# A three-layer field-interaction tower on one core: the first two blocks' layer-0 operands from TensorE, with a new order of the gathered rows

## The reference, cut to what matters

```python
e = jnp.stack([tbl_0[ids[:, 0]], ..., tbl_31[ids[:, 31]]], axis=1)   # 512 x 32 fields x 16
x0 = xk = e
for W in (W0, W1, W2):            # 32 x 32 x 64, then 32 x 64 x 64 twice
    xk = relu(einsum('bmd,bhd,mhk->bkd', x0, xk, W))
    outs.append(sum(xk, axis=2))
z = concatenate(outs, axis=1)
h = concatenate([z, dense_ctx], axis=1)
h = maximum(h @ W_top1 + b_top1, 0)
h = maximum(h @ W_top2 + b_top2, 0)
y = h @ W_top3
```

## Time and profile before

| | us |
|---|---|
| runs of the kernel | 358.14, 358.73, 359.80 (median 358.73) |
| the profiled execution | 356.49 |
| its span in the trace | 354.7 |
| PE busy | 294.3 (83%) |
| DVE busy | 274.4 (77%) |
| POOL busy | 255.2 (72%) |
| ACT busy | 57.2 (16%) |

### The profile page before, as it was taken

How to read it: one execution, slowest core, us unless ns; L and a number is a source line. 1 busy time by engine, 2 the same in 40 slices (tenths; PEclk the granted TensorE clock), 3 DMA queues, 4 the chain that set the end, 5 groups by cost and what they waited for, 6 DMA issues and landing times.

```text
span 354.7 us, 3875 instructions
## 1 busy us (share of the span) xinstructions
PE 294.3 (83%) x1452; PEld 117.3 (33%) x1452; DVE 274.4 (77%) x135; ACT 57.2 (16%) x73; POOL 255.2 (72%) x197
## 2 busy tenths in 40 slices
PE   0027596698997969997979899996999996999995
PEld 0004253353343324332334343431333332333341
DVE  0034497779977989998999999999499969899300
ACT  1000010210111220211212202113021022020031
POOL 5777778878888888777898798989941859963000
PEclk9999989999998999999999999998999999999999
DMA  5186878979149999694499997963998995230000
GB/s 179 24 255 174 252 190 268 333 250 303 29 136 309 324 370 311 212 311 123 115 307 348 324 305 267 325 192 84 314 340 314 291 331 164 37 96 2 6 10 0
DMA packets 35810, 75.57 MB, mean 213 GB/s; under 512 B 6000, under 2 KB 14192, under 8 KB 35792
## 3 DMA queue, kind: packets, MB, share of 16 engines
q1 hardware_dynamic: 24752, 61.68, 50.6%
q10 hardware_dynamic: 6944, 12.59, 13.0%
q0 software_dynamic: 4096, 1.06, 3.0%
HBM read 60.23 MB, written 2.10 MB: 176 GB/s over the span
## 4 chain that ended last, share of the span: by engine, by line
PE 38%; DMA 28%; DVE 11%; POOL 9%; issue 6%; SPq 3%; ACTq 1%; ACT 1%; DVEq 0%; POOLq 0%
PE acc L713 33%; DMA fields_sb<-fields 14%; DVE vz L572 11%; DMA rotated<-fields 7%; POOL gathered L489 6%; DMA fields<-gathered 3%; POOL pz L516 3%; DMA hidden<-relu_out 2%; PE factor L742 2%; DMA gathered<-in_table,index 1%; ACTq L641 1%; PE acc L709 1%; PE factor L736 1%; PE factor L683 1%; SPq L444 1%
## 5 line engine op out<-in xcount | busy, mean ns | idle before, releaser
L713 PE MATMUL acc<-vz,w_sb 128*64 128x512 f32 (+1 forms) x1068 | 224.9, 560 | 47.8 <-DVE vz L572 47.3
L572 DVE TENSOR_TENSOR vz<-fields_sb,factor 128x3072 f32<-128x3072 f32 (+3 forms) x92 | 225.1, 2490 | 23.0 <-PE acc L713 13.9
L516 POOL TENSOR_TENSOR pz<-fields_sb,hidden 128x1024 f32<-128x1024 f32 (+1 forms) x57 | 127.7, 2260 | 28.9 <-DMA fields_sb<-fields 11.0
L489 POOL DMA_INDIRECT gathered<-in_table,index x128 | 122.0, 953 | 35.1 <-issue 34.0
L713 PEld LDWEIGHTS acc<-vz,w_sb 128*64 128x64 f32 x1068 | 84.6, 143 | 174.6 <-issue 142.0
L713 PE MATMUL acc<-pz,w_sb 128*64 128x512 f32 (+1 forms) x228 | 56.9, 580 | 7.6 <-POOL pz L516 7.6
L572 DVE TENSOR_TENSOR vz<-rotated,factor 128x4096 f32<-128x4096 f32 (+2 forms) x13 | 36.1, 2778 | 28.9 <-DMA rotated<-fields 24.4
L606 ACT ACTIVATE factor<-hidden 128x1024 f32<-128x1024 f32 x24 | 24.7, 1028 | 106.9 <-DMA hidden<-relu_out 86.6
L632 ACT ACTIVATE relu_out<-acc 128x512 f32<-128x512 f32 (+1 forms) x27 | 14.8, 550 | 129.9 <-PE acc L713 78.3
L713 PEld LDWEIGHTS acc<-pz,w_sb 128*64 128x64 f32 x228 | 17.2, 137 | 38.0 <-issue 24.9
L582 DVE TENSOR_REDUCE feats<-relu_out 128x32 f32<-128x512 f32 (+1 forms) x27 | 16.7, 619 | 4.1 <-ACT relu_out L632 4.1
(11 more groups left out here) (17 smaller groups left out, 19.9 us busy)
## 6 DMA issues: line engine op xcount, KB each, us to landing
fields_sb<-fields SPq DMA_DIRECT2D x56, 512.0 KB, 6.8
rotated<-fields SPq DMA_DIRECT2D x28, 512.0 KB, 5.7
hidden<-relu_out ACTq DMA_DIRECT2D x48, 256.0 KB, 5.9
fields_sb<-fields SPq DMA_DIRECT2D x16, 256.0 KB, 3.9
own<-fields SPq DMA_DIRECT2D x7, 512.0 KB, 3.8
gathered<-in_table,index POOLq DMA_INDIRECT x128, 4.2
rotated<-fields SPq DMA_DIRECT2D x8, 256.0 KB, 3.5
fields<-gathered SPq DMA_DIRECT2D x14, 128.0 KB, 2.1
```

The source lines that it names most:

```text
L489: nc.gpsimd.indirect_dma_start(gathered[:, pair % GRING, j, :], None, table, bass.IndirectOffsetOnAxis(ap=index[:, i:i + 1], axis=0)).then ...
L516: nc.gpsimd.tensor_tensor(pz[:, at % PRING, 0:cols], fields[s][:, t, col:col + cols], hidden_of(step, g), ALU.mult).then_inc(pz_ready, 1)
L572: nc.vector.tensor_tensor(vz[:, at:at + nt, 0:cols].rearrange("p t (a n) -> p t a n", n=half), src[:, t:t + nt, col:col + cols].rearrange( ...
L713: last = nc.tensor.matmul(acc_of(step, ab), w_sb[layer][:, kt, :], z[:, ab * half:(ab + 1) * half], start=start and j == 0, stop=stop and ...
```

## The change

Blocks 0 and 1 (`DIRECT`) no longer read `own`, `opposite` and `rotated` back from DRAM. TensorE makes them in PSUM from `gathered` itself, with 0/1 matrices that hold the turn: `turned_sb` for the four rotated tiles, `across_sb` for the opposite one, `unit_sb` for the unturned rows (`OWN`). Each of the first five takes four matmuls of 32 rows by 128 columns in two waves, with a semaphore between the waves. ScalarE copies the unturned rows from PSUM to `own` in SBUF, and VectorE multiplies `own` by each turned tile: five products for such a step where there were four (the third and fourth tile were one product). The PSUM ring of three is now shared by six entries of each of these steps.

For this each quarter of the columns must lie on 32 partitions of its own. So in all blocks the partition of a gathered row is quarter * 32 + field, where it was field * 4 + quarter; the ids and `first_row` are permuted to fit, the DRAM side of the scratch writes of all blocks is walked quarter, field, columns, and the `opposite` read of blocks 2 to 8 fetches only the far field (128 KB, not 256 KB), walked the same way; GpSimd multiplies it by `gathered`. A gather that overwrites a buffer of `gathered` also waits for that product. The tables of the schedule (`BEGUN`, `GATHERS_IN`, `POOL_TILES`, `SPREAD`, `FIELDS_ORDER`) are as they were.

```diff
+DIRECT = (0, 1)
-        if b < 2:
-            return [(0, 0, 1), (0, 1, 1), (0, 2, 2), (0, L0TILES, 1)]
+        if b in DIRECT:
+            return [(0, t, 1) for t in range(L0TILES + 1)]
...
 def spread_after(step, g):
+    if spread_from_gathered(step):
+        return max(factor_free((step, g)), max(0, VECTOR.index((step, 0)) - 2))
     return max(factor_free((step, g)), min(vectors_to(source(step)) + 1, VECTOR.index((step, 0))))
...
+            sp.dma_start(unit_sb[:, :], unit).then_inc(unit_in, 16)
+            sp.dma_start(turned_sb[:, :, :], turned).then_inc(unit_in, 16)
+            sp.dma_start(across_sb[:, :], across).then_inc(unit_in, 16)
...
                     copy = fields_dram[b][c * FIELDS:(c + 1) * FIELDS, :]
-                    sp.dma_start(copy.rearrange("m (q x) -> (m q) x", q=QUART),
-                                 gathered[:, pair % GRING, first:first + rows, :].rearrange("p b d -> p (b d)")) \
+                    sp.dma_start(copy.rearrange("m (q x) -> q m x", q=QUART),
+                                 quarter_rows(b)) \
                       .then_inc(scratch_in[stream(b)][c], 16)
...
-                both = bass.AP(span.tensor, span.offset, [[quarter, P], [FIELDS // 2 * cols, 2], [1, quarter]])
-                sp.dma_start(opposite[s][:, :, col // QUART:col // QUART + quarter], both) \
-                  .then_inc(opposite_in[s], 16)
+                far = bass.AP(span.tensor, span.offset + FIELDS // 2 * cols,
+                              [[quarter, QUART], [cols, FIELDS], [1, quarter]])
+                sp.dma_start(opposite[s][:, :], far).then_inc(opposite_in[s], 16)
...
+                if b in DIRECT:
+                    for c in range(2):
+                        sp.wait_ge(scratch_in[s][c], landed(b))
...
-            for b in range(2):
+            for b in DIRECT:
                 scratch(b)
-                layer0_operands(b)
                 field_tiles(b)
...
                     for c in range(2):
                         pool.wait_ge(scratch_in[stream(before)][c], landed(before))
+                    if before in DIRECT:
+                        pool.wait_ge(vz_ready, vectors_to((0, before)))
+                    else:
+                        pool.wait_ge(pz_ready, pools_to((0, before)))
...
+            def direct_product(step, t, at):
+                _, col, cols, _, _ = BLOCKS[step[1]]
+                half, quarter = cols // 2, cols // QUART
+                dve.wait_ge(factor_spread, SPREADS.index((step, t)) + 1)
+                if t == L0TILES:
+                    nc.vector.tensor_tensor(vz[:, at, 0:quarter], quarter_rows(step[1]),
+                                            factor_of(step, t)[:, 0, 0:quarter], ALU.mult).then_inc(vz_ready, 1)
+                    return
+                dve.wait_ge(own_copied, DIRECT.index(step[1]) + 1)
+                nc.vector.tensor_tensor(vz[:, at, 0:cols].rearrange("p (a n) -> p a n", n=half),
+                                        own[stream(step[1])][:, col:col + cols].rearrange("p (a n) -> p a n", n=half),
+                                        factor_of(step, t), ALU.mult).then_inc(vz_ready, 1)
...
+            def copy_own(step):
+                _, col, cols, _, _ = BLOCKS[step[1]]
+                act.wait_ge(factor_spread, SPREADS.index((step, OWN)) + 1)
+                nc.scalar.activation(own[stream(step[1])][:, col:col + cols].rearrange("p (a n) -> p a n", a=2),
+                                     factor_of(step, OWN), ACT.Copy).then_inc(own_copied, 1)
...
+            def spread_gathered(step, g):
+                b = step[1]
+                rows, quarter = quarter_rows(b), BLOCKS[b][2] // QUART
+                if factor_free((step, g)):
+                    pe.wait_ge(vz_ready, factor_free((step, g)))
+                if g == L0TILES:
+                    nc.tensor.matmul(factor_of(step, g)[:, 0, 0:quarter], across_sb[:, :], rows,
+                                     start=True, stop=True).then_inc(factor_spread, 1)
+                    return
+                pe.wait_ge(rows_in[b], 16 * BLOCKS[b][4])
+                for wave in range(2):
+                    if wave:
+                        pe.wait_ge(wave_done, SPREAD_WAVES.index((step, g)) + 1)
+                    for ab in range(2):
+                        q = 2 * ab + wave
+                        row = slice(q * FIELDS, (q + 1) * FIELDS)
+                        by = unit_sb[row, :] if g == OWN else turned_sb[row, g, :]
+                        last = nc.tensor.matmul(factor_of(step, g)[:, ab, wave * quarter:(wave + 1) * quarter],
+                                                by, rows[row, :], start=True, stop=True)
+                    last.then_inc(factor_spread if wave else wave_done, 1)
```

More of the change, by code:

```diff
@@ L98, in pool_units @@
     if layer == 0:
-        return [(0, L0TILES)] if b > 1 else []
+        return [(0, L0TILES)] if b not in DIRECT else []
     return [(1, t) for t in range(TILES - POOL_TILES[step], TILES)]
@@ L143, in tensor_program @@
             program += mine
[L144 to L147, removed]
+    for step, g in FACTORS:
+        if step in SPREAD or spread_from_gathered(step):
+            after = spread_after(step, g)
+            made = VECTOR[after - 1]
+            at = program.index((made[0], "v", made[1])) + 1 if after else 0
             while program[at][1] == "spread":
@@ L164, in source, with spread_from_gathered, factor_entry, factor_entries @@
     return step[0] - 1, step[1]
[L168 to L170 removed]
+def spread_from_gathered(step):
+    return step[0] == 0 and step[1] in DIRECT
+OWN = L0TILES + 1
+def factor_entry(step, u):
+    g, t, _ = vector_units(step)[u]
+    return step, t if spread_from_gathered(step) else g
+def factor_entries():
+    entries = []
+    for step, u in VECTOR:
+        if u == 0 and spread_from_gathered(step):
+            entries.append((step, OWN))
+        entries.append(factor_entry(step, u))
+    return list(dict.fromkeys(entries))
+FACTORS = factor_entries()
+FACTOR_USED = [max(i for i, (step, u) in enumerate(VECTOR)
+                   if factor_entry(step, u) == entry or entry == (step, OWN) and u == 0) + 1
                for entry in FACTORS]
@@ L206 @@
 SPREADS = [(step, g) for step, who, g in TENSOR if who == "spread"]
+SPREAD_WAVES = [(step, g) for step, g in SPREADS if spread_from_gathered(step) and g != L0TILES]
 COPIED = [step for step in BEGUN if step in SPREAD and pool_units(step)]
@@ L296, in cin_dlrm @@
         rotated = [sb(f"rotated{s}", [P, L0TILES, PAIR]) for s in range(STREAMS)]
-        opposite = [sb(f"opposite{s}", [P, 2, PAIR // QUART]) for s in range(STREAMS)]
+        opposite = [sb(f"opposite{s}", [P, PAIR // QUART]) for s in range(STREAMS)]
         fields = [sb(f"fields_sb{s}", [P, TILES, PAIR]) for s in range(STREAMS)]
@@ L363, in hidden_of, with quarter_rows, operands_in @@
             return hidden[stream(step[1])][:, g, col:col + cols]
+        def quarter_rows(b):
+            pair, _, _, first, rows = BLOCKS[b]
+            return gathered[:, pair % GRING, first:first + rows, :].rearrange("p b d -> p (b d)")
+        def operands_in(b):
+            return 16 * sum(1 for a in range(b + 1) if a not in DIRECT and stream(a) == stream(b))
         def landed(b):
@@ L551, in product @@
                     dve.wait_ge(vz_used, free)
-                if layer == 0 and t == L0TILES:
-                    quarter = cols // QUART
-                    part = slice(col // QUART, col // QUART + quarter)
-                    dve.wait_ge(opposite_in[s], landed(b))
-                    nc.vector.tensor_tensor(vz[:, at, 0:quarter], opposite[s][:, 0, part], opposite[s][:, 1, part],
-                                            ALU.mult).then_inc(vz_ready, 1)
+                if spread_from_gathered(step):
+                    direct_product(step, t, at)
                     return
@@ L566, in product @@
                     if layer == 0:
-                        dve.wait_ge(rotated_in[s][tile], landed(b))
+                        dve.wait_ge(rotated_in[s][tile], operands_in(b))
                     elif layer == 1 and g == 0:
@@ L647, in _ @@
                     put_factor(step, g)
+                elif what == "own":
+                    copy_own(step)
                 elif what == "copy":
```

51 lines of the change are left out of this document (32 added, 19 removed).

## The result

The changed kernel took 362.28 us (median of 20 runs, 358.39 to 365.59) where the kernel before took 357.92 beside it (20 runs). The ratio is 1.0106, with a 95% interval of 1.007 to 1.0141: slower by 3.8 us, 2.5 to 5.0. The ratio leaves out each kernel's slow runs, those over 1.5% above its fastest, one of 1084.16 us of the kernel before among them, and so is smaller than that of the two medians (4.4 us). The profiled execution took 360.12 us with a span of 358.3, 3.6 more than before.

A forecast was written before the change was run, and what follows sets the result against it. No single limit: the start held by GpSimd's program order, the end by DMA. 356.5 - 0.4 + 1.8 + 3.1 = 361.0 us profiled; against the median 358.7 + 4.5 = 363.2, stated as 363.0, range 360.6 to 366.

The forecast's parts named there:

- Four engines: Quarter-first scratch and `opposite` copies run on four of 16 DMA engines: +2.3 and +0.8, together +3.1 us per large block.
- Exposed at blocks 7 and 8, 3.1 us: From block 8's scratch to (1,8) the chain is DMA, so all 3.1 us per block count.
- Exposed at blocks 5 and 6, 1.8 us: Later field tiles delay the products of (1,5) by 1.3 to 2.1 us; 1.8 taken.
- The start, -0.4 us: At block 2, (0,2) waits for ScalarE's put instead of its tiles: 65.3 instead of 65.72, a gain of 0.4 us.
- the wall: GpSimd's 40 gathers before its products of (1,1) keep those at 53.93 and 57.61, whatever finishes earlier.
- TensorE's 58.94, the relu at 63.10 and the put until 65.24 stay: Behind GpSimd's unmoved (1,1) products, TensorE's contraction, the relu and ScalarE's put for (0,2) keep their times.
- Block 0's estimate of 31 us for the spread of (1,0): With 9 us of waves, the spread comes at 31 us against 29.87 before: no gain, perhaps a microsecond lost.
- The sum: Whole kernel: -0.4 at the start, +1.8 at blocks 5 and 6, +3.1 at blocks 7 and 8; +4.5 us.
- Sixteen engines anyway: Rival: copies are dealt to 16 engines as before, -0.8 us in all, 357.9 us; chance 0.20.
- The start's gain gets through: Rival: (0,2) starts as its tiles land, up to 7 us earlier, some 5 survive, about 354 us; chance 0.09.
- Hidden: Rival: four engines, but block 6's 1.8 us absorbed and part of 3.1 covered by `own`; 359.8 us; chance 0.07.
- Hurt everywhere: Rival: nothing hidden in saturated stretches after 100 us, or start waves use up the cover; 369 us; chance 0.06.

The follow-up runs named there:

- e1: Kernel before with only the quarter-first partition order and scratch walk of all blocks; ratio 1.0156 to the kernel before.
- e2b: Changed kernel with old partition order, scratch walk and `opposite` read for blocks 2 to 8, run again; 355.81 us, ratio 0.9973 to the kernel before.
- e5: Changed kernel with every quarter-first copy cut into four DMAs of 32 partitions, same addresses; ratio 1.0513 to the kernel before, in a slow-starting round.
- e4b: Changed kernel with nine unused 512-column matmuls before TensorE's wait for GpSimd's first product of (1,1), second run; ratio 1.02 to the kernel before.
- e3: Changed kernel with six gathers moved from before GpSimd's first product of (1,1) to behind (0,2); ratio 1.0367 to the kernel before, slow-starting round.
- e23: Kernel of e2 with six gathers moved from before GpSimd's first product of (1,1) to behind (0,2); ratio 1.034 to the kernel before, slow-starting round.
- e2: Changed kernel with old partition order, scratch walk and `opposite` read for blocks 2 to 8; ratio 1.0191 to the kernel before, in a slow-starting round.

## Why the prediction was right

- **Four engines: right, in kind and size.** Forecast +2.3 us for the second copy, share near 0.25; measured at least +2.5, 0.27 to 0.28 over full microseconds. e1 shows that this part alone makes the loss, e2b that without it there is none, e5 that the addresses are not the cause.
- **Exposed at blocks 7 and 8, 3.1 us:** 2.9 in the mean of the traces. In the single pair of profiles it doesn't show: -0.4 from the scratch of block 8 to the end. The kernel before lost time there too: its (1,8) waited 3.53 us for a tile, the changed one's 1.57, while tiles of (1,7) held it for 1.33 and TensorE for 2.37.
- **Exposed at blocks 5 and 6, 1.8 us: wrong place, size not settled.** I had it at the last field tile of (1,5); GpSimd's wait there grew only from 0.76 to 0.97. In the changed kernel it was paid one step earlier, +2.0, by the hidden rows' relay, which runs beside the later field tiles and holds ScalarE's put of (0,6). I had left the relay out of the list of DMAs that come later. The mean over traces, +1.8, rests on three whose wait is unexplained; without them it is +0.8. That it meets the forecast is luck.
- **The start, -0.4 us: the wall was right, the sum was not.** GpSimd's products did not move, and the put decided when (0,2) began. What failed is the step "TensorE's 58.94, the relu at 63.10 and the put until 65.24 stay": work that finishes earlier in front of a wall leaves TensorE idle in front of it, and in the profiled execution the clock was at 0.50 when it went on. The put ended 2.7 us later than that step said, and the start came out at +2.3 us. Over runs only e2b speaks, whose start differs in block 2's walk: -0.27% (-0.62% to +0.08%), about -1 us, with the forecast inside and zero too. Block 0's estimate of 31 us for the spread of (1,0) was too long: it stood at 27.55, since a wave in the early stage took about 0.65 us and TensorE worked on the next entry while VectorE multiplied.
- **The sum.** Forecast +4.5 us by the median, measured +3.8 (2.5 to 5.0). By means: -1.0 + 1.8 + 2.9 = +3.7, of which the first can't be told from zero and the second is unsure. In the single pair of profiles the terms are others: +2.3 at the start, +2.0 to (0,6), -0.4 from there to the scratch of block 8 and -0.4 behind it, +3.6 in all. A start 2.7 us dearer than forecast and an end 3.5 us cheaper cancelled there. What carries the forecast is the price of the walk, 4.9 us exposed against 4.7 (3.0 to 6.5) between the changed kernel and e2b; how it is shared out between the stages is not shown.
- **The rivals.** Sixteen engines anyway: out. The start's gain gets through: out; scratch of block 2 went 4.3 us earlier (45.49 against 49.77), and that ended in front of GpSimd's products. Hidden: out. Hurt everywhere: blocks 0 to 4 hid it, as the constant 2.33 us from (0,2) to (0,5) shows.

## What to carry to other kernels

When a layout changes, look at the outermost dimension of every DMA that touches it, on both sides: three lines that only reorder rows and a view cost 1.3 to 1.7%, where all that the new matmuls of the change gave back was 0.27%, not to be told from nothing. A DMA share that sits flat at 4/16 while one copy runs is the sign to look for. And before an early stage is made faster, name the fixed order behind it that it will run into: here 40 gathers, and behind them a TensorE that stood idle and went on at a granted clock of 0.50. Last, a sum that comes out right is not yet right in its terms: look at each stage, and at more than one pair of profiles.

## What the runs showed of the hardware that was not expected

- TensorE's granted clock was 0.50 at different places of nearly the same start. In the changed kernel and in e2b it fell at 30.3 us, behind 5 us in which TensorE was busy for 3.1. In the changed kernel it was back at 33.7 and fell again from 54.2 to 64.5, in and behind a wait of 4.39 us; in e2b it stayed at 0.50 until 50.6, in a stretch in which TensorE was busy for 4.9 of each 5 us. The kernel before showed 0.66 from 45 to 50 and from 245 to 250. What holds it at 0.50 in the busy stretch stays open.
- The clock column and the durations do not always agree. Up to 30 us the changed kernel's column shows 1.00, yet four records of 256 columns take 1.12 us there (18.91 and 22.51), as at 0.50 later; in e4b it is so up to 50 us. So costs are better read from durations.
- In the slow-starting rounds, on three chips, TensorE, VectorE or ScalarE stood in the first 70 us, released by nothing that the trace shows: in e1 ScalarE for 40.44 us before its first relu, in e3 TensorE for 15.77 and 15.92 and VectorE for 15.73 and 21.57. In e3 and e23 it came again at 100 to 111 us, 10.7 us on VectorE. Kernels with the new start lost more there (e2 1.0191 where e2b had 0.9973); the cause was not tested.
